# One core of Trainium2, graph attention layer: the last six supersteps of the second edge loop in another order

## The chip, the cores and the metric

The kernel runs on one core of one Trainium2 chip. The time is that of one execution on the device, in microseconds (us). Three executions of the kernel before took 5511.41 us in the median (5510.93 to 5514.28). All times inside the program are counted from the first instruction of one profiled execution.

## What is computed

Two graph layers over 12500 nodes with 64 features and 200000 edges, sorted by destination. The change lies in the second, an attention layer with eight relations:

```python
Z = jnp.einsum('ni,rio->nro', h, fc_weight)
z_s = Z[src, etype]
z_d = Z[dst, etype]
aw = attn_weight[etype, :, 0]
z2 = jnp.concatenate([z_s, z_d], axis=1)
e = jax.nn.relu(jnp.sum(z2 * aw, axis=1))
m = jax.ops.segment_max(e, dst, num_segments=N)
ex = jnp.exp(e - m[dst])
denom = jax.ops.segment_sum(ex, dst, num_segments=N)
alpha = ex / denom[dst]
h_out = jax.ops.segment_sum(alpha[:, None] * z_s, dst, num_segments=N)
```

The first layer is a message layer with `segment_sum` over the same edges. Each layer is followed by an addition of its input and a normalisation.

## The kernel before

The 200000 edges make 1563 tiles of 128. Nodes lie in 98 blocks of 128. Since the edges are sorted, a tile meets one block or a few, and the work is a row of (tile, block) slots, eight to a **superstep**: 208 supersteps (`SO`), 196 groups of eight tiles. Everything is unrolled.

**Gathers.** In each of the two layers GpSimd (POOL) fetches the source rows of each tile by one indirect DMA (`gathers`, L466) into a ring of 184 tiles. It reports each landed group in the semaphore `landed`, and may run on only when the compute side has freed old ring places (`used`, `summed`).

**The second loop** (`phase_layer1`). For the data of superstep s each engine does, in its own fixed program order:

- `onehots(s)` on VectorE (DVE): one-hot matrices of the slots' destinations (L1399, L1401, L1404).
- `scores(s)` on TensorE (PE): sixteen small matmuls (L1340, L1345) into the bank `p_e`; the first L1345 waits for `landed` against a register loaded from the table `xrow`. Then `scores(s)` on DVE (L1410, L1414) makes the logits `ev`.
- `scored(s)` on ScalarE (ACT): one-hot times logit, `ohe` (eight, L1315). `turned(s)` on PE transposes them (eight, L1351) into `p_x`.
- `maxima(s)` on DVE: a reduction (L1424) and a running maximum, split in three bf16 parts `m` (L1427 to L1441). `spread(s)` on PE brings the maxima back to the edges (eight small matmuls, L1357). They land in the last 24 columns of the bank `p_s` of the odd half (`pB`).
- `shifted(s)` on DVE: logit minus maximum, `ed` (L1460, L1462). `weights(s)` on ACT: exponentials and eight weighted one-hots `ohx` (L1305, L1306, L1309).
- `summed(s, h)` on PE: two halves of four f32 matmuls each against the ring (L1366), into `p_s`; `sums(s)` on DVE: eight additions into the accumulator XA (L1454), each waiting for the one ahead of it.

I call a pass of an engine's loop a **turn**. In turn s PE does turned(s-1), scores(s+1), summed(s-3, 0), spread(s-1), summed(s-3, 1). DVE does scores(s), onehots(s+2), then maxima(s-1) and sums(s-4) woven instruction by instruction, then shifted(s-2). ACT does scored(s), weights(s-2). So the data of the last superstep, 207, are added in turn 211.

```python
for s in range(SO + 4):
    if s < SO:
        scores(s)
    if s + 2 < SO:
        onehots(s + 2)
    weave(*([maxima(s - 1)] if 1 <= s <= SO else []), *([sums(s - 4)] if s >= 4 else []))
    if 2 <= s < SO + 2:
        shifted(s - 2)
```

After this loop all engines meet at a barrier, and `phase_out` scales, normalises and stores the result; its first DVE instruction is L1513. The first layer's loop (`phase_layer0`) has the same gathers; there DVE waits for `landed` ahead of L875, against a register of the four that it loads at L899.

Of the kernel before, what the change touches and what calls it, by code (L numbers as in the profile page):

```python
# [17 lines left out]
R = 8  # L18
# [465 lines left out]
def phase_layer0(nc, A):  # L484
# [4 lines left out]
    with ExitStack() as ctx:  # L489
# [268 lines left out]
        def _(e):  # L758
            breg = [e.alloc_register(f"l0vb{j}") for j in range(O)]
            treg = [e.alloc_register(f"l0vt{j}") for j in range(O)]  # L760
            xreg = [e.alloc_register(f"l0vx{j}") for j in range(WX)]
            done = Chain(e, T["dve"])
# [107 lines left out]
            def filled(s):  # L870
                e.wait_ge(S["landed"], e.snap(xreg[0], min_val=1, max_val=TO))
                if s:
                    e.wait_ge(S["pre"], s)
                of, to = e.snap(xreg[1], min_val=0, max_val=RING - O), e.snap(xreg[2], min_val=0, max_val=O)
                e.tensor_tensor(out=full[:, bass.ds(to, O), :], in0=owns, in1=ring[:, bass.ds(of, O), :], op=ALU.add).then_inc(S["full"], 1)  # L875
# [11 lines left out]
            for s in range(SO + 2):  # L887
                if s + 1 < SO:
                    onehots(s + 1)
                if s < SO:  # L890
                    if s:
                        e.wait_ge(S["msg"], s)
                    for h in range(2):
                        e.wait_ge(S[f"m{h}"], s + 1)
                        e.tensor_reduce(out=pT[:, h * H:(h + 1) * H, :], in_=half(h), axis=AXX, op=ALU.add).then_inc(T["dve"], 1)  # L895
                if s >= 2:
                    e.reg_load(breg, A.brow[0:1, (s - 2) * O:(s - 1) * O])
                if s < SO:
                    e.reg_load(xreg, xrow[0:1, s, :])  # L899
                    e.reg_load(treg, wrow[0:1, s, :])  # L900
                    filled(s)
                    take(e, T["dve"], 2)
                for j in range(O):
                    if s >= 2:
                        summed(s - 2, j)
                    if s < SO:
                        added(s, j)
# [341 lines left out]
def phase_layer1(nc, A):  # L1249

    QO, QT, QV = 7, 5, 4
    with ExitStack() as ctx:
# [26 lines left out]
        pE = pb("p1_e", [P, O, 3 * R])  # L1279
# [3 lines left out]
        pB = [pair[1][:, 512 - 3 * O:512].rearrange("p (j c) -> p j c", c=3) for pair in p_s]  # L1283
        names = "oht e ev ohe x m3 b ed ohx s0 s acc dve ex ty landed".split()
# [16 lines left out]
        def _(e):  # L1301
# [16 lines left out]
            for s in range(SO + 2):  # L1318
                if s < SO:
                    scored(s)  # L1320
                if s >= 2:
                    weights(s - 2)

        @block.tensor
        def _(e):
# [3 lines left out]
            xreg = e.alloc_register("l1px")  # L1329

            def scores(s):
                e.reg_load(breg, A.brow[0:1, s * O:(s + 1) * O])
                e.reg_load(treg, trow[0:1, s, :])
                e.reg_load(xreg, xrow[0:1, s, 0:1])
                e.wait_ge(S["oht"], s + 1)
                if s:
                    e.wait_ge(S["ev"], s)
                for j in range(O):
                    b = e.snap(breg[j], min_val=0, max_val=NB)
                    e.matmul(pE[:, j, :], OHT[:, s % QT, j, :], A.S23[:, bass.ds(b, 1), :], start=True, stop=False)  # L1340
                    if j == 0:
                        e.wait_ge(S["landed"], e.snap(xreg, min_val=1, max_val=TO))
# [11 lines left out]
            def spread(s):  # L1354
                e.wait_ge(S["m3"], s + 1)
                for j in range(O):
                    last = e.matmul(pB[s % 2][:, j, :], OHT[:, s % QT, j, :], m3[:, s % 2, j, :], start=True, stop=True)  # L1357
# [12 lines left out]
            for s in range(SO + 3):  # L1370
                if 1 <= s <= SO:
# [3 lines left out]
                if s >= 3:  # L1375
                    summed(s - 3, 0)
                if 1 <= s <= SO:
                    spread(s - 1)
                if s >= 3:
                    summed(s - 3, 1)  # L1380

        @block.vector
        def _(e):
# [74 lines left out]
            def shifted(s):  # L1458
                e.wait_ge(S["b"], s + 1)
                step(e.tensor_reduce(out=md[:, :], in_=pB[s % 2], axis=AXX, op=ALU.add))  # L1460
# [7 lines left out]
            for s in range(SO + 4):  # L1468
# [4 lines left out]
                weave(*([maxima(s - 1)] if 1 <= s <= SO else []), *([sums(s - 4)] if s >= 4 else []))  # L1473
                if 2 <= s < SO + 2:
                    shifted(s - 2)
# [248 lines left out]
```

## Time and profile before

| what | value |
|---|---|
| median of three executions | 5511.41 us |
| span of the profiled execution, first to last instruction | 4190.6 us |
| own time of the profiled execution | not recorded; the median is 1320.8 us more than the span |
| first loop's gathers | 30.7 to 1993.3 us |
| second loop's gathers | 2151.0 to 4106.1 us |
| last addition of the second loop ends | 4153.2 us |
| output phase | 4153.5 to 4190.6 us |
| busy over the span: PE / PE weight loads / DVE / ACT / POOL | 77 / 68 / 71 / 30 / 72 % |
| mean granted TensorE clock | 0.52 of full |

Busy shares are averages over stages with different limits. What counts for a stage is which wait ends last in it. The profile infers who released a wait from semaphore events, and matmul ends are modelled.

### The profile page before, as it was taken

To read this page: it belongs to the slowest core of one execution; us is meant where nothing else is said; L and a number is where in the kernel's file an instruction comes from. 1 tells how busy PE (TensorE), PEld (TensorE's weight loads), DVE (VectorE), ACT (ScalarE), POOL (GpSimd) and SP (SyncE) were. 2 spreads that over 40 slices of the span, in tenths; PEclk is the share of its full clock that TensorE was granted. 3 is DMA by queue.
4 is the path that set the end of the run, shared out by engine and by line. 5 is a ranking of instruction groups with operands and counts; after the bars stand their busy time and mean duration, and the time that the engine had idled before them with its cause. 6 is when DMAs were issued, how large, how long until landed. Compare 5 with 4: busy or idle time off the path is not lost. (4 is left out here: it accounts for less than half of the span.)

```text
span 4190.6 us, 74370 instructions
## 1 busy us (share of the span) xinstructions
PE 3206.3 (77%) x17849; PEld 2851.7 (68%) x17849; DVE 2985.6 (71%) x9486; ACT 1278.0 (30%) x4181; POOL 3029.9 (72%) x3265
## 2 busy tenths in 40 slices
PE   6877677777677777777857877787878888888885
PEld 6766666667666766666626767676777777777774
DVE  6876676677677777777656666676767777777777
ACT  3000000000000000000334544555555555555555
POOL 5777777777777777777257777777777777777773
PEclk6555555555555555555775555555555555555555
DMA  5322222222222222222452222222222222222221
GB/s 187 104 71 71 60 71 71 69 63 72 70 71 72 65 69 71 72 71 62 151 209 59 49 59 49 59 59 59 49 59 59 59 59 49 59 59 59 59 49 37
DMA packets 172566, 300.35 MB, mean 72 GB/s; under 512 B 71720, under 2 KB 78236, under 8 KB 158845
## 3 DMA queue, kind: packets, MB, share of 16 engines
q0 software_dynamic: 100032, 105.03, 12.7%
q1 hardware_dynamic: 43526, 104.29, 6.9%
q10 hardware_dynamic: 28598, 86.26, 6.0%
q8 instruction: 173, 2.83, 0.3%
q14 instruction: 237, 1.93, 0.2%
HBM read 260.36 MB, written 34.99 MB: 70 GB/s over the span
## 5 line engine op out<-in xcount | busy, mean ns | idle before, releaser
L466 POOL DMA_INDIRECT ring<-Btab,idx x1563 | 1485.5, 950 | 504.6 <-issue 338.9
L466 POOL DMA_INDIRECT ring<-Ztab,idx x1563 | 1478.9, 946 | 485.6 <-issue 352.8
L1366 PE MATMUL p_s<-ring,ohx 128*128 x3328 | 806.3, 421 | 160.5 <-issue 157.0
L1366 PEld LDWEIGHTS p_s<-ring,ohx 128*128 128x128 f32 x3328 | 734.7, 325 | 180.8 <-issue 180.8
L754 PEld LDWEIGHTS p_s<-msg,oh 128*128 128x128 f32 x3328 | 726.2, 331 | 99.8 <-issue 99.7
L754 PE MATMUL p_s<-msg,oh 128*128 128x64 f32 x3328 | 756.9, 422 | 48.4 <-ACT msg L648 45.8
L741 PE MATMUL p_m<-A,oht 128*128 x1664 | 436.1, 364 | 411.0 <-DVE full L875 401.7
L648 ACT ACTIVATE msg<-p_t 128x512 f32<-128x512 f32 x208 | 124.2, 597 | 1803.8 <-DVE p_t L881 1790.9
L746 PE MATMUL p_m<-W1c,eaT 65*128 65x128 f32 x1664 | 573.9, 449 | 24.4 <-DMA eaT<-in_eaT_in 24.4
L741 PEld LDWEIGHTS p_m<-A,oht 128*128 128x128 bf16 x1664 | 233.4, 141 | 490.4 <-issue 444.4
L1454 DVE SCALAR_TENSOR_TENSOR XA<-XA,ff,p_s 128x65 f32 x1664 | 468.4, 281 | 129.9 <-DVE XA L1454 73.1
L1424 DVE TENSOR_REDUCE mslot<-p_x 128x8 f32<-128x1024 f32 x208 | 254.7, 1224 | 429.1 <-PE p_x L1351 427.7
L1315 ACT ACTIVATE ohe<-oh,ev 128x128 f32<-128x128 bf16 x1664 | 505.3, 386 | 44.6 <-DVE ev L1414 44.6
L1309 ACT ACTIVATE ohx<-oh,ex 128x128 f32<-128x128 bf16 x1664 | 508.7, 388 | 0.0
L1345 PE MATMUL p_e<-ring,ident_h 128*128 x1664 | 303.4, 196 | 234.2 <-POOLq L453 226.5
L746 PEld LDWEIGHTS p_m<-W1c,eaT 65*128 65x128 f32 x1664 | 455.9, 334 | 33.4 <-DMA eaT<-in_eaT_in 27.7
L875 DVE TENSOR_TENSOR full<-p_m,ring 128x512 f32 x208 | 143.6, 690 | 448.9 <-POOLq L453 430.3
L1351 PE MATMUL p_x<-ident,ohe 128*128 128x128 f32 x1664 | 397.6, 418 | 0.0
L1345 PEld LDWEIGHTS p_e<-ring,ident_h 128*128 128x128 bf16 x1664 | 166.6, 105 | 336.4 <-issue 274.0
L881 DVE TENSOR_TENSOR p_t<-p_t,full 128x64 f32<-128x64 f32 x1664 | 386.2, 233 | 11.7 <-issue 6.3
L868 DVE TENSOR_TENSOR XA<-XA,p_s 128x64 f32 x1664 | 366.9, 221 | 36.2 <-issue 8.5
L895 DVE TENSOR_REDUCE p_t<-p_m 128x256 f32<-128x768 f32 x416 | 379.5, 956 | 13.9 <-PE p_m L746 13.1
(212 smaller groups left out, 3084.4 us busy)
## 6 DMA issues: line engine op xcount, KB each, us to landing
drow<-drow_d SPq DMA_DIRECT2D x53, 1024.0 KB, 5.4
drow<-drow_d ACTq DMA_DIRECT2D x51, 1024.0 KB, 5.2
eaT<-in_eaT_in ACTq DMA_DIRECT2D x208, 128.0 KB
Ztab<-Z_stage SPq DMA_DIRECT2D x49, 536.0 KB, 5.5
ring<-Btab,idx POOLq DMA_INDIRECT x1563
ring<-Ztab,idx POOLq DMA_INDIRECT x1563
xTB<-in_xTB_in SPq DMA_DIRECT2D x7, 448.0 KB, 7.7
Btab<-B_stage SPq DMA_DIRECT2D x7, 448.0 KB, 5.1
```

What stands on the lines that cost most here:

```text
L466: e.indirect_dma_start(out=ring[:, place(t), :], out_offset=None, in_=table[:, :], in_offset=bass.IndirectOffsetOnAxis(ap=idx[:, t:t + 1], ...
L741: e.matmul(parts(j), OHT[:, s % 2, j, :], A.A3[:, bass.ds(b, 1), :].rearrange("p a c -> p (a c)"), start=True, stop=True)
L746: last = e.matmul(own(j // 2), eaT[:, s % QE, j // 2, :], A.W1c2[:, :], start=True, stop=True)
L754: last = e.matmul(pS[r % 2][:, j, :], OH[:, r % QO, j, :], msg[:, r % 2, j, :], start=True, stop=True)
L881: ins = e.tensor_tensor(out=pT[:, j:j + 1, :], in0=pT[:, j:j + 1, :], in1=full[:, bass.ds(t, 1), :], op=ALU.add)
L895: e.tensor_reduce(out=pT[:, h * H:(h + 1) * H, :], in_=half(h), axis=AXX, op=ALU.add).then_inc(T["dve"], 1)
L1309: ins = e.activation(OHx[:, o, j, :], OH[:, s % QO, j, :], ACT.Copy, scale=ex[:, o, j:j + 1])
L1315: ins = e.activation(OHe[:, s % 2, j, :], OH[:, s % QO, j, :], ACT.Relu, scale=ev[:, s % QV, j:j + 1])
L1345: last = e.matmul(pE[:, j, :], A.ident_h[:, :], part.unsqueeze(2).to_broadcast([P, 3, R]), start=False, stop=True)
L1351: last = e.transpose(pX[:, j, :], OHe[:, s % 2, j, :], A.ident[:, :])
L1366: last = e.matmul(pS[s % 2][h][:, j % 4, :], OHx[:, s % 2, j, :], ring[:, bass.ds(t, 1), 0:D + 1], start=True, stop=True)
L1454: e.scalar_tensor_tensor(out=acc, in0=acc, scalar=ff[:, s % QV, j:j + 1], in1=pS[s % 2][j // 4][:, j % 4:j % 4 + 1, :], op0=ALU.mult, op1= ...
```

## The change

**Order.** `END = SO - 6` = 202. Up to turn 201 nothing moves. From turn 202 on, sums, their matmuls and their weights run one superstep closer behind the scores:

- DVE: in turn 202 sums(198) alone first. In each turn then shifted(s-2), scores(s), onehots(s+2), and maxima(s-1) woven with sums(s-3). The last turn is 210.
- ACT: weights(s-2) ahead of scored(s), where it stood behind it.
- PE: turn 202 has summed(199) and summed(200), from there summed(s-2). In turns 208 and 209 both halves of summed(s-2) stand together, in turn 208 behind spread(207).
- From data 201 on, spread writes to free columns of the bank of `p_e`, and shifted reads them there.

**Registers.** In both loops the count that `landed` is compared with is first copied to a register of its own (REGISTER_ALU): on DVE in the first loop, on PE in the second, once a superstep, 208 each.

```diff
@@ phase_layer0, DVE
+            landed = e.alloc_register("l0vn")
...
-                e.wait_ge(S["landed"], e.snap(xreg[0], min_val=1, max_val=TO))
+                e.wait_ge(S["landed"], e.snap(landed, min_val=1, max_val=TO))
...
                     e.reg_load(xreg, xrow[0:1, s, :])
+                    e.reg_alu(landed, xreg[0], 0, ALU.max)
                     e.reg_load(treg, wrow[0:1, s, :])
@@ phase_layer1
+    END = SO - 6
-        pE = pb("p1_e", [P, O, 3 * R])
+        p_e = ctx.enter_context(nc.psum_tensor("p1_e", [P, 512], F32))
+        pE = p_e[:, 0:O * 3 * R].rearrange("p (a b) -> p a b", b=3 * R)
+        pBE = p_e[:, O * 3 * R:O * 3 * R + 3 * O].rearrange("p (j c) -> p j c", c=3)
+        spreads = lambda s: pB[s % 2] if s < END - 1 else pBE
@@ ACT
             for s in range(SO + 2):
+                if s >= END:
+                    weights(s - 2)
                 if s < SO:
                     scored(s)
-                if s >= 2:
+                if 2 <= s < END:
                     weights(s - 2)
@@ PE
                 e.reg_load(xreg, xrow[0:1, s, 0:1])
+                e.reg_alu(landed, xreg, 0, ALU.max)
...
+            for s in range(END, SO + 2):
+                if s <= SO:
                     turned(s - 1)
                 if s + 1 < SO:
                     scores(s + 1)
-                if s >= 3:
-                    summed(s - 3, 0)
-                if 1 <= s <= SO:
+                if s == END:
+                    for h in range(2):
+                        summed(s - 3, h)
+                if s < SO:
+                    summed(s - 2, 0)
+                if s <= SO:
                     spread(s - 1)
-                if s >= 3:
-                    summed(s - 3, 1)
+                if s >= SO:
+                    summed(s - 2, 0)
+                summed(s - 2, 1)
@@ DVE
+            for s in range(END, SO + 3):
+                if s == END:
+                    for _ in sums(s - 4):
+                        pass
+                if s < SO + 2:
+                    shifted(s - 2)
                 if s < SO:
                     scores(s)
                 if s + 2 < SO:
                     onehots(s + 2)
-                weave(*([maxima(s - 1)] if 1 <= s <= SO else []), *([sums(s - 4)] if s >= 4 else []))
-                if 2 <= s < SO + 2:
-                    shifted(s - 2)
+                weave(*([maxima(s - 1)] if s <= SO else []), sums(s - 3))
```

**DVE at the end of the loop, before.** In the rows below L1460 and L1462 are shifted, each L1444 opens a group of eight additions (a load of eight registers, then pairs of L1452 and L1454, of which the first is shown).

```order
L1460 TENSOR_REDUCE md<-p_s 128x8 [waits l1_b]
L1462 SCALAR_TENSOR_TENSOR ed<-ev,md 128x8 [waits l1_ty]
L1444 TENSOR_LOAD tabs
L1452 ISA [waits l1_acc,l1_s0]
...
L1460 TENSOR_REDUCE md<-p_s 128x8 [waits l1_b]
L1462 SCALAR_TENSOR_TENSOR ed<-ev,md 128x8 [waits l1_ty]
L1444 TENSOR_LOAD tabs
L1452 ISA [waits l1_acc,l1_s0]
...
L1444 TENSOR_LOAD tabs
L1452 ISA [waits l1_acc,l1_s0]
...
L1252 UNCONDITIONAL_BRANCH
```

Here sums(205) stands between shifted(206) and shifted(207), and sums(206) and sums(207) follow. The same place in the changed program:

```order
L1484 TENSOR_REDUCE md<-p_e 128x8 [waits l1_b]
L1486 SCALAR_TENSOR_TENSOR ed<-ev,md 128x8 [waits l1_ty]
L1468 TENSOR_LOAD tabs
L1476 ISA [waits l1_acc,l1_s0]
...
L1468 TENSOR_LOAD tabs
L1476 ISA [waits l1_acc,l1_s0]
...
L1255 UNCONDITIONAL_BRANCH
```

The shift shown is shifted(207): only two groups of additions are left behind it, sums(206) and sums(207). shifted(206) has moved ahead of maxima(207).

**PE at the same place, changed.** L1361 is turned(207), L1367 spread(207), L1376 summed.

```order
L1361 MATMUL p_x<-ident,ohe 128x128 [waits l1_ohe]
L1361 MATMUL p_x<-ident,ohe 128x128 x7
L1367 MATMUL p_e<-m,oht 128x3 [waits l1_m3]
L1367 MATMUL p_e<-m,oht 128x3 x7
L1372 TENSOR_LOAD tabs
L1375 ISA [waits l1_ohx]
L1376 MATMUL p_s<-ring,ohx 128x65
```

Before, the first half of summed(205) stood between turned(207) and spread(207), its second half behind, and summed(206) and summed(207) followed; now only summed(206) and summed(207) follow.

**DVE at the seam, turn 202, changed.** The last of eight additions of sums(198), then shifted(200), scores(202) and the one-hots.

```order
L1476 ISA [waits l1_acc]
...
L1484 TENSOR_REDUCE md<-p_s 128x8 [waits l1_b]
L1486 SCALAR_TENSOR_TENSOR ed<-ev,md 128x8 [waits l1_ty]
L1434 TENSOR_TENSOR prod<-p_e,ty 128x192 [waits l1_oht,l1_e]
L1438 TENSOR_REDUCE ev<-prod 128x8 [waits l1_ty]
L1423 TENSOR_TENSOR oh<-p_iota,dstl 128x1024
```

Before, the scores (L1410, L1414) opened the turn, and sums(198) was woven with maxima(201).

## Rows read from the trace of the kernel before

**Rows 1.** Windows: busy us (instructions) of PE, PEld, DVE, ACT, POOL; granted clock; DMA.
```profile
2151.00:4106.00 1955.00, 1548.15 (x9767) 1381.52 (x9767) 1366.27 (x4724) 1023.34 (x3661) 1478.74 (x1563) 0.51 0.23 57
4106.00:4153.50 47.50, 36.84 (x218) 34.18 (x218) 28.91 (x115) 23.13 (x84) 0.12 (x1) 0.50 0.01 2
4153.50:4190.60 37.10, 0.00 (x0) 0.00 (x0) 31.82 (x46) 20.10 (x57) 23.98 (x12) 0.50 0.38 86
```
**Rows 2.** POOL, gathers: count, min/median/max ns, first to last start; then the last.
```profile
L466 POOL DMA_INDIRECT ring<-Ztab,idx x1556: 940/944/1205, 2159.8 to 4105.2; - x195
...
L466 POOL DMA_INDIRECT ring<-Ztab,idx x23: 940/944/947, 4077.7 to 4105.2; - x23
...
4105.18 0.94 POOL L466 DMA_INDIRECT ring<-Ztab,idx  x1 [0.30 <-DVE XA L1454]
```
**Rows 3.** Waits over the second loop, then one over the first: us, times, longest.
```profile
PE p_e L1345 <- POOLq L453: 226.5, 129, 5.8
...
POOL ring L466 <- DVE XA L1454: 73.1, 240, 0.3
...
DVE full L875 <- POOLq L453: 430.3, 156, 4.3
```
**Rows 4.** Timeline of PE in the last turns: start, us, instruction, idle before it.
```profile
4080.82 1.91 PE L1351 MATMUL p_x<-ident,ohe 128*128 128x128 f32 x8
...
4094.09 0.20 PE L1345 MATMUL p_e<-ring,ident_h 128*128 x1 [1.37 <-POOLq L453]
...
4100.79 1.91 PE L1351 MATMUL p_x<-ident,ohe 128*128 128x128 f32 x8
...
4104.02 0.20 PE L1345 MATMUL p_e<-ring,ident_h 128*128 x1 [1.30 <-POOLq L453]
...
4110.79 1.91 PE L1351 MATMUL p_x<-ident,ohe 128*128 128x128 f32 x8
...
4112.49 0.23 PE L1340 MATMUL p_e<-S,oht 128*128 x1
...
4114.28 1.96 PE L1366 MATMUL p_s<-ring,ohx 128*128 x8 [0.79 <-issue]
...
4118.13 1.91 PE L1351 MATMUL p_x<-ident,ohe 128*128 128x128 f32 x8
...
4133.33 1.91 PE L1351 MATMUL p_x<-ident,ohe 128*128 128x128 f32 x8
...
4138.68 0.37 PE L1357 MATMUL p_s<-m,oht 128*128 128x3 bf16 x8 [1.02 <-DVE m L1441]
...
4143.13 3.67 PE L1366 MATMUL p_s<-ring,ohx 128*128 x16 [2.26 <-ACT ohx L1309]
...
4147.58 3.67 PE L1366 MATMUL p_s<-ring,ohx 128*128 x16 [0.78 <-ACT ohx L1309]
```
**Rows 5.** Timeline of DVE in the same stretch.
```profile
4102.74 1.23 DVE L1424 TENSOR_REDUCE mslot<-p_x 128x8 f32<-128x1024 f32 x1 [2.60 <-PE p_x L1351]
...
4135.28 1.22 DVE L1424 TENSOR_REDUCE mslot<-p_x 128x8 f32<-128x1024 f32 x1 [2.44 <-PE p_x L1351]
...
4140.09 0.17 DVE L1462 SCALAR_TENSOR_TENSOR ed<-ev,md 128x8 f32<-128x8 f32 x1
...
4140.95 0.28 DVE L1454 SCALAR_TENSOR_TENSOR XA<-XA,ff,p_s 128x65 f32 x1 [0.69 <-issue]
...
4144.55 0.17 DVE L1462 SCALAR_TENSOR_TENSOR ed<-ev,md 128x8 f32<-128x8 f32 x1
...
4149.71 0.28 DVE L1454 SCALAR_TENSOR_TENSOR XA<-XA,ff,p_s 128x65 f32 x1 [0.83 <-PE p_s L1366]
...
4152.90 0.28 DVE L1454 SCALAR_TENSOR_TENSOR XA<-XA,ff,p_s 128x65 f32 x1 [0.16 <-DVE XA L1454]
```
**Rows 6.** Timeline of ACT: the last weighting.
```profile
4144.99 2.44 ACT L1309 ACTIVATE ohx<-oh,ex 128x128 f32<-128x128 bf16 x8
```
**Rows 7.** Timeline of DVE: the last superstep of the first loop.
```profile
2005.39 0.69 DVE L875 TENSOR_TENSOR full<-p_m,ring 128x512 f32 x1 [0.66 <-issue]
```

More of the change, by code:

```diff
@@ L1329, in _ @@
             xreg = e.alloc_register("l1px")
+            landed = e.alloc_register("l1pn")
             def scores(s):
@@ L1341, in scores @@
                     if j == 0:
-                        e.wait_ge(S["landed"], e.snap(xreg, min_val=1, max_val=TO))
+                        e.wait_ge(S["landed"], e.snap(landed, min_val=1, max_val=TO))
                     t = e.snap(treg[j], min_val=0, max_val=RING - 1)
@@ L1356, in spread @@
                 for j in range(O):
-                    last = e.matmul(pB[s % 2][:, j, :], OHT[:, s % QT, j, :], m3[:, s % 2, j, :], start=True, stop=True)
+                    last = e.matmul(spreads(s)[:, j, :], OHT[:, s % QT, j, :], m3[:, s % 2, j, :], start=True, stop=True)
                 last.then_inc(S["b"], 1)
@@ L1369, in _ @@
             scores(0)
-            for s in range(SO + 3):
-                if 1 <= s <= SO:
+            for s in range(END):
+                if s:
+                    turned(s - 1)
+                scores(s + 1)
+                if s >= 3:
+                    summed(s - 3, 0)
+                if s:
+                    spread(s - 1)
+                if s >= 3:
+                    summed(s - 3, 1)
+            for s in range(END, SO + 2):
+                if s <= SO:
                     turned(s - 1)
@@ L1374, in _ @@
                     scores(s + 1)
-                if s >= 3:
-                    summed(s - 3, 0)
-                if 1 <= s <= SO:
+                if s == END:
[4 more added lines that the diff above has]
+                if s <= SO:
                     spread(s - 1)
-                if s >= 3:
-                    summed(s - 3, 1)
+                if s >= SO:
+                    summed(s - 2, 0)
+                summed(s - 2, 1)
         @block.vector
@@ L1459, in shifted @@
                 e.wait_ge(S["b"], s + 1)
-                step(e.tensor_reduce(out=md[:, :], in_=pB[s % 2], axis=AXX, op=ALU.add))
+                step(e.tensor_reduce(out=md[:, :], in_=spreads(s), axis=AXX, op=ALU.add))
                 stepped()
@@ L1467, in _ @@
             onehots(1)
-            for s in range(SO + 4):
+            for s in range(END):
+                scores(s)
+                onehots(s + 2)
+                weave(*([maxima(s - 1)] if s else []), *([sums(s - 4)] if s >= 4 else []))
+                if s >= 2:
+                    shifted(s - 2)
[4 more added lines that the diff above has]
+                if s < SO + 2:
+                    shifted(s - 2)
                 if s < SO:
```

## Prediction

> **What bounds the kernel now.** I read the windows by stage first, then the gathers, the waits, and last the timelines of the final turns, engine by engine. The windows give three stretches that matter: 1955 us in which the second loop's gathers run, 47.5 us of the loop behind the last gather, and 37.1 us of output [rows 1]. In the first, POOL is the bound: 1563 gathers in 1955 us are 1.251 us each, 0.944 us of work and some 0.30 us of issue, so eight take 10.0 us [rows 1, 2]. POOL waits for the additions 240 times, and never for more than those 0.3 us [rows 3]; nothing the compute side does sets its pace. PE, in turn, waits 226.5 us in this loop for landed groups, and DVE 430.3 us in the first loop [rows 3]. The timeline of PE shows the same at the end: transposes start 10.0 us apart (4100.79, 4110.79; two turns earlier 4080.82), with 1.30 to 1.37 us of waiting for a landed group in a turn, the last one at 4104.02 [rows 4]. From there the pace is that of the compute engines: the next transposes are 7.34 us apart (4110.79, 4118.13) [rows 4]. So a paced turn has 10.0 - 7.34 = 2.66 us to spare on PE. DVE has as much: it sits idle 2.60 us ahead of the maxima [rows 5].
>
> The last maxima start at 4135.28 [rows 5]. Behind them come only leftovers of the pipeline: two shifts, and sums(205), (206) and (207), one after the other on DVE, until 4152.90 + 0.28 = 4153.18 [rows 5]. Only the stretch behind the last landed group can give the change anything.
>
> **Term 1, the end of the loop: a gain of 4.3 us.** The last chain before is: shift(207) at 4144.55, ScalarE's one-hots from 4144.99 (2.44 us), summed(207) on PE from 4147.58, first addition at 4149.71, last end 4153.18 [rows 4 to 6]. Shift(207) stood behind sums(205) because that group lay between the two shifts. The group with its load of registers and the shift costs 4144.55 - 4140.09 = 4.46 us [rows 5]. In the new order sums(205) is woven with maxima(207), in the place where sums(204) was, and shift(206) stands ahead of maxima(207), where DVE was idle for 2.44 us [rows 5] and the shift of some 0.4 us fits. So shift(207) lands at about 4140.09, where shift(206) was, and the whole chain moves up 4.46 us, if PE is free for it. PE is nearly the limit: spread(207) starts at 4138.68 as before and takes some 0.25 us until the next may start; then come a load of registers, which stands in the open for about 0.79 us [rows 4], and both halves of a superstep's sums, 3.67 us to the last end and some 3.5 until the next may start [rows 4]. That is 4138.68 + 0.25 + 0.79 + 3.5 = 4143.2 for the end of summed(206). The weights of 207 are there at 4144.99 + 2.44 - 4.46 = 4143.0 [rows 6]. PE then starts summed(207) at 4143.2 to 4143.3 if the second load of registers hides behind the matmuls; from there to the first addition it takes 4149.71 - 4147.58 = 2.13 us, and eight additions 4153.18 - 4149.71 = 3.47 us [rows 4, 5]: end at 4148.9. The gain is 4.3 us; 3.5 if the second load stands in the open as well. I take 4.3, since behind eight f32 transposes PE's next matmul starts at 4112.49 without a gap, loads and all [rows 4].
>
> **Term 2, the seam: a loss of 0.1 us.** Turn 202 gets work twice. On PE an extra summed: 3.5 us and a load of 0.79 make 4.3. On DVE the additions of sums(198), 3.47 us, stand alone ahead of the shift and the scores; of a shift there is no more than before in any turn. PE has 2.66 us to spare in each of the turns 203 and 204, 5.3 us together, before the last group for which it waits has landed at 4104.02, and 4.3 is less. DVE has its 2.60 us of idle time in the same two turns, 5.2 us against 3.47 [rows 5]. So turned(204) should start at 4110.79 again and maxima(203) a little later than 4102.74. Since each of the two waits for the other while both are late, a rest may stay. I count 0.1. Bounds: nothing, or the whole extra 4.3 if none of it is caught up.
>
> **Term 3, the tail's five turns: nothing.** The pace of 7.34 us is PE's own: the same matmuls in the same order, with another superstep's number on the sums. The new order asks ScalarE for weights(s-2) ahead of scored(s): twice eight activations of 2.44 us together [rows 6] and two small ones, some 5.2 us a turn, under 7.34. From the end of the maxima over spread (0.25), shift (0.4), weights (2.7) and half a sum (1.75) to the next spread is 5.1 us of work, under 7.34 too. The waits that stay are for the maxima.
>
> **Term 4, the register copies: a loss of 0.2 us.** 208 on DVE in the first loop and 208 on PE in the second. No row shows a copy. From below: it gains nothing, as nothing is taken away. From above: a load of eight registers in the open, which costs 0.66 us on DVE and 0.79 on PE [rows 4, 7]; a copy that has to wait for its load can make at most such a gap. In the paced turns any of these lies in PE's 1.3 us and DVE's wait for a landed group [rows 3, 4]. Not covered are the last two supersteps of each loop, four copies: 0 to 3.0 us. A single register operation is nearer to the small steps between matmuls than to a load, so I take 0.05 each.
>
> **Sum.** -4.3 + 0.1 + 0 + 0.2 = -4.0 us. The barrier and the output phase behind it move up unchanged, since DVE's last addition is what the barrier waits for. The sum is made against the one profiled span: 4190.6 becomes 4186.6. That execution's own time isn't recorded; the 1320.8 us between the span and the median of 5511.41 lie outside the program's instructions and I leave them as they are. Forecast: 5507.4 us. A measurement of this kernel can tell 0.2%, or 11 us, from no change; this gain is 0.07%.
>
> **Rivals.** (a) **The seam isn't caught up**, because DVE's burst also holds up the gathers. Against it: the 23 gathers from 4077.7 to 4105.2 took 940 to 947 ns each with additions, reductions and one-hots running beside them, and the longest in the loop was 1205 ns [rows 2]. The group landed at 4104.02 would come later by what the eight moved additions cost, at most 8 x 0.28 = 2.2 us; with the seam's own delay the gain falls to between 0 and 3 us: 5508.5 to 5511.5. The Trainium skill's page "SBUF — State Buffer" ("SBUF: two separate sides") has a rule for this: VectorE and GpSimd share a port pair under an exclusive lock, and GpSimd can't write descriptors of its DMAs while VectorE holds it. By that rule POOL would be held up; the 940 to 947 ns in this trace show no such hold.
>
> (b) **The register copy makes PE wait for its loads in every superstep**, the one that ends slower. PE's scores of each superstep would then sit out a fixed c, ahead of the landed wait. PE's cover is 226.5 us over some 201 supersteps, 1.13 us each [rows 3]. Below that nothing happens but in the tail; above it PE takes over from POOL as the bound of the loop, at (c - 1.13) x 201. At c = 1.3 that is +34 us, less 4: 5541. It decides at c = 1.15, where the loss is as large as the gain. Against it: the load of eight registers shows 0.79 us [rows 4], and PE waits for its first block register at that place today already. The Trainium skill's page "Runtime: NRT & Kernel Launch" ("Instruction fetch mechanics") puts a register load at about 200 ns a register: 17 registers would be 3.4 us, and by it the kernel would be far slower. The 0.79 us for eight in this trace, with the issue in it, is under 0.1 each.
>
> (c) **Nothing changes**, since another chain sets the end. The barrier waits for all engines, but PE's last sixteen matmuls are through at 4147.58 + 3.67 = 4151.25, ahead of DVE's last addition, and POOL has been idle since 4106 [rows 2, 4, 5]. Then 5511.4.
>
> (d) **The tail gets faster by a turn**: one turn less at 7.34 us would be 5504. Against it: the turns up to the last maxima are as many as before; only leftovers go.
>
> **Chances.** Forecast, 3 to 4.5 us gained: 0.70. (a): 0.14. (b), with over 11 us lost: 0.03. (c): 0.06. (d): 0.04. Others, such as code that lies elsewhere after 416 more instructions: 0.03. Range: the forecast's bounds reach from 5507.0 to 5508, rivals (a) and (c) to 5511.5, (d) to 5504; the three executions before lie between 0.5 us under and 2.9 us over their median. That makes 5503.5 to 5512.5. Faster by over 0.2% would need 11 us, more than all the tail's leftovers of one superstep: 0.02. Slower by over 0.2% is (b) and a bit: 0.04. Same: 0.94.
>
> **What the new profile would show.** The last gather starts at 4105.2 again, within 1 us; else (a). The last group that PE waits for is released at about 4104, and the last maxima start at 4135.3, within 0.5 us: seam caught up. In turn 202 eight additions stand alone ahead of a shift, at 4079 to 4083. Behind the last maxima: one shift at 4140.1, then two groups of additions, the last beginning at about 4145.4 and ending at 4148.9; summed(206) and summed(207) almost without a gap on PE. PE's waits for landed groups in the second loop stay near 226 us, or fall by under 10; if they fall by half or more, the copies cost. I am wrong if the last maxima come later than 4137, or if the wait for landed groups is gone.

## The result, and the profile after

The changed kernel took **5535.18 us** (median of 4 executions, 5529.65 to 5541.09), the kernel before, run beside it, 5511.17 us. The ratio is **1.0046**, 95% interval 1.0035 to 1.0058: 24 us slower, by more than 0.2% and outside my range. The profiled execution took 5529.65 us itself and its span is 5527.9 us. So 1.75 us lie around the program, not the 1320.8 us that I had left outside it. Beside [rows 1], its windows (us; then busy us and instructions of PE, PEld, DVE, ACT, POOL; granted clock; DMA): the second loop's start, POOL's pause behind it, the rest of the gathers, and the loop behind the last gather.

```profile
2938.00:3166.00 228.00, 20.28 (x128) 15.69 (x128) 21.64 (x46) 13.75 (x43) 172.33 (x182) 0.50 0.19 37
3166.00:3230.00 64.00, 35.39 (x249) 33.20 (x249) 34.73 (x122) 25.22 (x90) 0.00 (x0) 0.50 0.05 18
3230.00:5330.00 2100.00, 1283.43 (x8701) 1167.83 (x8700) 1198.54 (x4216) 909.92 (x3263) 1305.31 (x1379) 0.51 0.20 47
5330.00:5490.00 160.00, 133.90 (x911) 124.10 (x909) 125.28 (x453) 97.56 (x351) 0.00 (x0) 0.53 0.04 15
```

The gathers of both loops, beside [rows 2]: count, min/median/max ns, first to last start.

```profile
L466 POOL DMA_INDIRECT ring<-Btab,idx x1563: 942/947/2037, 30.7 to 2638.7; - x196
L466 POOL DMA_INDIRECT ring<-Ztab,idx x1563: 942/947/1210, 2935.0 to 5326.8; - x196
```

One gather is as long as before (947 ns), the granted clock the same (0.51). Yet the first loop's gathers last 2608 us instead of 1963, the second's 2392 instead of 1955, and 160 us of the loop lie behind the last gather, not 47.5. By e1 and e3 below, this is not the effect of the change: the profile that I was shown came from a chip on which the same program is faster. Its waits (us, times, longest), beside [rows 3]:

```profile
POOL ring L466 <- issue: 773.9, 2526, 1.2
POOL ring L466 <- remote: 359.9, 172, 2.3
POOL ring L466 <- DVE XA L869: 345.9, 87, 5.3
POOL ring L466 <- SPq L443: 290.8, 158, 3.2
```
```profile
DVE oh L853 <- remote: 940.1, 88, 12.4
DVE mslot L1448 <- remote: 875.5, 174, 42.4
DVE full L876 <- POOLq L453: 2.0, 1, 2.0
```
```profile
PE p_e L1355 <- POOLq L453: 2.3, 1, 2.3
```

POOL now really waits for the compute side. The waits for landed groups in which I had hidden the copies, 226.5 us on PE and 430.3 on DVE [rows 3], are gone: 2.3 and 2.0 us. "remote" here is a wait that ended with a semaphore event, but so long behind every instruction that could have caused it that the view names none. The timeline at the second loop's start shows it: PE, then DVE.

```profile
2981.15 0.20 PE L1355 MATMUL p_e<-ring,ident_h 128*128 x1
3002.87 0.37 PE L1367 MATMUL p_s<-m,oht 128*128 128x3 bf16 x8 [21.51 <-issue]
3003.10 1.95 PE L1361 MATMUL p_x<-ident,ohe 128*128 128x128 f32 x8
3045.43 0.20 PE L1350 MATMUL p_e<-S,oht 128*128 x1 [40.39 <-issue]
```
```profile
3044.43 0.36 DVE L1434 TENSOR_TENSOR prod<-p_e,ty 128x192 f32<-128x192 f32 x1 [41.62 <-remote]
...
3089.24 1.22 DVE L1448 TENSOR_REDUCE mslot<-p_x 128x8 f32<-128x1024 f32 x1 [42.40 <-remote]
```

The transposes of 3003.10 end at 3005.05, and the event that DVE waits for is recorded at 3089.21. DVE, idle for 41.6 us, takes up the scores 63 us after PE's last score matmul (2981.35 to 3044.43), and, idle for another 42.4, the maxima 84 us after the transposes (3005.05 to 3089.24), while POOL issues gather after gather. Later, in the steady part, POOL and DVE:

```profile
4010.36 0.94 POOL L466 DMA_INDIRECT ring<-Ztab,idx  x1 [0.30 <-issue]
4013.41 0.95 POOL L466 DMA_INDIRECT ring<-Ztab,idx  x1 [2.10 <-remote]
```
```profile
4013.26 1.22 DVE L1448 TENSOR_REDUCE mslot<-p_x 128x8 f32<-128x1024 f32 x1 [4.59 <-remote]
```

PE's transposes for those maxima had ended at 4008.76 by the same trace, but DVE starts within 0.15 us of POOL's restart, behind 2.1 us without a gather. Eight gathers of 1.25 us and one such pause make the turn of some 12 us (11.6 to 12.0 from 3900 to 4019 us). In the unpaced turns behind the last gather it is 7.3 to 7.9 us.

### The profile page after: what moved, and what is told of

Read it like the earlier page. It is cut to its first block and busy times, and to the rows that moved or that the text cites. A ratio compares the mean times of both kernels' runs of the same rounds, so it can differ in the third digit from the quotient of the medians.

```text
span 5527.9 us, 74786 instructions
## 1 busy us (share of the span) xinstructions
PE 3115.1 (56%) x17849; PEld 2801.3 (51%) x17849; DVE 2984.1 (54%) x9486; ACT 1278.0 (23%) x4181; POOL 3032.0 (55%) x3265
## 5 line engine op out<-in xcount | busy, mean ns | idle before, releaser
L754 PE MATMUL p_s<-msg,oh 128*128 128x64 f32 x3328 | 785.0, 409 | 755.7 <-issue 719.4
L754 PEld LDWEIGHTS p_s<-msg,oh 128*128 128x128 f32 x3328 | 752.7, 325 | 806.4 <-issue 805.4
L1376 PE MATMUL p_s<-ring,ohx 128*128 x3328 | 811.1, 421 | 184.1 <-issue 184.1
L1376 PEld LDWEIGHTS p_s<-ring,ohx 128*128 128x128 f32 x3328 | 740.4, 326 | 208.0 <-issue 207.5
L853 DVE TENSOR_TENSOR oh<-p_i,dstl 128x1024 f32<-128x1024 f32 x208 | 253.6, 1219 | 948.3 <-remote 940.1
L1350 PE MATMUL p_e<-S,oht 128*128 x1664 | 216.1, 191 | 391.3 <-issue 348.3
L1361 PE MATMUL p_x<-ident,ohe 128*128 128x128 f32 x1664 | 397.8, 418 | 0.8 <-issue 0.8
L1355 PE MATMUL p_e<-ring,ident_h 128*128 x1664 | 220.9, 186 | 286.0 <-issue 282.8
```

Source lines behind the costliest of these rows:

```text
L754: last = e.matmul(pS[r % 2][:, j, :], OH[:, r % QO, j, :], msg[:, r % 2, j, :], start=True, stop=True)
L1361: last = e.transpose(pX[:, j, :], OHe[:, s % 2, j, :], A.ident[:, :])
L1376: last = e.matmul(pS[s % 2][h][:, j % 4, :], OHx[:, s % 2, j, :], ring[:, bass.ds(t, 1), 0:D + 1], start=True, stop=True)
```

## Experiments

The cores came from several chips, each with the kernel before run beside: its median was 4192 us on one of them, 5512, 5513 and 5513 on three, 5575 and 5601 on two. I call these levels. Each ratio is against the kernel before on the same chip.

**Copies alone, and the changed kernel, at the 4192 level.** `e1_copies_only` has the old order and the copies of the diff in both loops; `e2_copies_three` has each of them three times in its source, both engines (VectorE's shown); `e3_changed_again` is the changed kernel.

```diff
@@ e2, against e1
                     e.reg_alu(landed, xreg[0], 0, ALU.max)
+                    e.reg_alu(landed, xreg[0], 0, ALU.max)
+                    e.reg_alu(landed, xreg[0], 0, ALU.max)
```

> The kernel before with only the 416 register copies; the order of the last six supersteps is the old one. Theory A (the copies cost the 24 us, some 0.06 us each, since the compute engines and not the gathers set the pace in the timed executions): 5530 to 5537 us, ratio 1.004 to 1.005. Theory B (the new order costs it, at the seam or in the tail): 5509 to 5514, ratio 1.000. The profile should also tell whether a kernel in the old order spans 4191 us, as the profile of before did, or some 5510 us with stretches in which PE sits idle on nothing that the profile shows, as in the changed kernel's.

> As the first, with each copy made three times (1248 in all instead of 416). Theory A: the cost grows with the number, to three times that of the first, about +70 us over the kernel before. Theory B: within 3 us of the first.

> The changed kernel unchanged, on the same chip. Both theories: ratio 1.0046 again, 5530 to 5540 us. Against the first run it gives the cost or gain of the order alone: theory A says equal to it or up to 4 us less; theory B says 20 to 26 us more.

Measured: 4192.53, 4192.62 and 4187.64 us against 4191.86; ratios 1.0000 and 1.0000 (each 0.9991 to 1.0009), and 0.9989 (0.9980 to 0.9998). So at this level the copies cost nothing that can be told, and the change gains 4.2 us (0.8 to 8). Of three copies e2 says nothing: its trace holds 74786 instructions, exactly as e1's does, 416 more than the kernel before (74370). Two of three equal copies, each of which only writes the same value again, aren't in the compiled program. The same holds for e10 and e17 below. The changed kernel's timeline there, PE and DVE, answers [rows 4, 5]:

```profile
4080.21 1.91 PE L1361 MATMUL p_x<-ident,ohe 128*128 128x128 f32 x8
4087.02 5.38 PE L1376 MATMUL p_s<-ring,ohx 128*128 x24 [0.76 <-issue]
...
4094.19 1.91 PE L1361 MATMUL p_x<-ident,ohe 128*128 128x128 f32 x8
...
4101.56 1.91 PE L1361 MATMUL p_x<-ident,ohe 128*128 128x128 f32 x8
...
4138.59 7.25 PE L1376 MATMUL p_s<-ring,ohx 128*128 x32 [0.41 <-issue]
```
```profile
4134.40 1.23 DVE L1448 TENSOR_REDUCE mslot<-p_x 128x8 f32<-128x1024 f32 x1 [2.44 <-PE p_x L1361]
...
4139.14 0.17 DVE L1486 SCALAR_TENSOR_TENSOR ed<-ev,md 128x8 f32<-128x8 f32 x1
...
4148.04 0.28 DVE L1478 SCALAR_TENSOR_TENSOR XA<-XA,ff,p_s 128x65 f32 x1 [0.16 <-DVE XA L1478]
```

Turn 202 is 14.0 us long (4080.21 to 4094.19), and the last maxima still come 29.8 us behind the last gather's start (4104.6), before 30.1: the seam is caught up. The last addition ends 13.9 us behind the start of the last maxima (4148.32 - 4134.40), before 17.9 [rows 5].

**The order at the 5601 level.** `e4_old_order` is the kernel of e1; `e5_end3` and `e6_end14` are the changed kernel with a shorter and a longer new stretch (`SO - 3` and `SO - 14`).

```diff
-    END = SO - 6
+    END = SO - 3
```

> The old order with the copies again. Its time against the kernel before tells which of the two levels this chip shows. If 4190 us: ratio 1.000, as the first run. If 5510 us: by theory C (at that level the copies cost nothing either, the 24 us are the seam and the tail, where the compute engines run behind the gathers and have no slack to catch up in) 5509 to 5514; by theory A (copies) 5530 to 5537; and its profile shows PE stopping in every superstep while gathers run.

> The changed kernel with the switch three supersteps before the end instead of six (turn 205), behind the last group that PE waits for. My working: the extra sums of the turn of the switch, 4.3 us on PE, then find no slack; from the trace's steps I get a loss of 2 us against the old order, where the switch in turn 202 gains 4. At the 4190 level: 4193 to 4195 us, ratio 1.0005. If the seam were free, 4187.6 as with the changed kernel. At the 5510 level theory C expects the same as, or a little more than, the changed kernel.

> The switch fourteen supersteps before the end (turn 194), in the midst of the gathers. At the 4190 level the seam lies further inside the slack: 4187 to 4188 us, as the changed kernel or up to 1 us better. At the 5510 level, theory C: no better than the changed kernel, since there the compute engines run behind throughout and a seam costs the same wherever it stands.

Measured against 5601.43: 5610.38 (1.0016, 1.0005 to 1.0028), 5615.47 (1.0023, 1.0014 to 1.0033) and 5619.05 us (1.0036, 1.0024 to 1.0048). In the traces the seam's turn is 14.7 us in e5 and 15.3 in e6, where its neighbours are 7.3 to 8.0, and from the start of the last transposes to the end of the last addition it is 15.9 and 16.0 us instead of 19.8 in e4. At this level some 18 turns are left when the last gather has been issued, so that the seam lies in unpaced turns in e5 and e6 alike: it costs 7 to 8 us, and the end gives back 4. But the old order with copies is 9 us above the kernel before as well (3 to 16), so the order isn't all of it.

**Old order, changed kernel, a gentler seam, and sixteen copies on PE in the source, at the 5513 level.** `e7_old_order` and `e8_changed` are the two kernels again. In `e9_gentle_seam` VectorE does the scores ahead of the lone additions in turn 202, and ScalarE moves its weights one turn later; `e10_pe16` has the old order with PE's copy sixteen times in its source.

```diff
@@ e9, DVE
                 if s == END:
+                    scores(s)
                     for _ in sums(s - 4):
                         pass
@@ e10, PE
-                e.reg_alu(landed, xreg, 0, ALU.max)
+                for _ in range(16):
+                    e.reg_alu(landed, xreg, 0, ALU.max)
```

> The anchor of this comparison: the old order with the copies. On a chip of the 4190 level 1.000 of the kernel before. On one of the 5500 to 5600 level 1.000 to 1.003, as in the fourth run; what the next runs differ from it by is the order's part alone.

> The changed kernel. Level 4190: 4 us less than the old order. Level 5500: theory C (PE has no slack there, the turn of the switch costs 8 us and the end gives back 4) says 3 to 5 us more than the old order with the copies; theory A (all is in the copies) says 0 to 4 us less.

> The changed kernel with another turn 202: DVE does scores(202) ahead of the lone sums(198), and ACT scored(202) ahead of weights(200), so that PE's next scores need not wait 3.3 us for the logits. Level 4190: as the changed kernel, within 1 us. Level 5500: 2 to 3 us less than the changed kernel, so about the old order's time, since the pace there is PE's own.

> The old order, but PE's copy of each superstep in the second loop made sixteen times (3120 instructions more on PE's queue alone). Level 4190: PE has 1.1 us of slack a superstep; at a few hundredths of a us each fifteen copies fit in it, ratio 1.000 (theory E: a copy costs up to 0.1 us, then 0.4 us a superstep over the slack, +80 us). Level 5500, where PE's semaphore updates reach DVE only once the gathers pause: if each PE instruction adds to what has to be worked off in that pause (theory D), +30 to +140 us; if only the pause's length counts, under 15 us.

Measured against 5513.0: 5532.72 (1.0035, 1.0021 to 1.0048), 5531.35 (1.0036, 1.0022 to 1.0050), 5532.22 (1.0038, 1.0025 to 1.0052) and 5538.26 us (1.0051, 1.0035 to 1.0066). Two things follow. The copies in the old order already cost 20 us, about the whole loss of the change. The order adds nothing that can be told: from the last gather's start to the end of the span it is 201.4 us in e8 and 198.2 in e7, 3 us more, which drowns in the few us between executions. The gentler seam makes turn 202 11.6 us long, not 15.7, and that stretch 198.1 us; the time is the same. What a copy costs when there are more of them e10 can't tell, since its program has 74786 instructions, as e7's has. PE's copy in e7, and then all that is left in e10 of the sixteen (count; min/median/max ns):

```profile
L1338 PEldq ALU_OP  x208: 32/33/47, 2947.5 to 5465.5; - x104
```
```profile
L1339 PEldq ALU_OP  x208: 32/33/47, 2942.7 to 5459.8; - x104
```

So e10 is a repetition of e7, and the second loop's gathers take as long in both (2392.2 and 2393.1 us).

**Which copy.** `e11_old_order_2` is the anchor (old order, both copies). `e12_const_first` has a constant as the count in the first loop, so only PE's copy; `e13_const_second` the other way round. The constant is never under what the register holds, and binds nowhere here, since the gathers are far ahead of the compute side (the wait for landed groups is 2 us in the whole loop). `e14_late_copy` puts VectorE's copy behind the load of the slot registers. The compiled programs differ by more than the copies: with the constant, VectorE's move of the count (one MOVE a superstep) is gone too in e12, and in e13 PE's move and its load of the count, which nothing uses any more. In e14 the copy and the move have become one instruction.

```diff
@@ e12, DVE, first loop (e13: PE, second loop)
-                e.wait_ge(S["landed"], e.snap(landed, min_val=1, max_val=TO))
+                e.wait_ge(S["landed"], min(s + 1, TO))
...
-                    e.reg_alu(landed, xreg[0], 0, ALU.max)
@@ e14
                     e.reg_load(xreg, xrow[0:1, s, :])
-                    e.reg_alu(landed, xreg[0], 0, ALU.max)
                     e.reg_load(treg, wrow[0:1, s, :])
+                    e.reg_alu(landed, xreg[0], 0, ALU.max)
```

> The old order with the register copies in both loops, as anchor for the three beside it. Where the kernel before takes about 5510 us: 1.0035 of it (19 us more), as in the earlier run of this kernel; where it takes about 4190: 1.0000.

> Old order; in the first loop VectorE waits for the constant min(s + 1, 196) in place of a register, without a copy; in the second PE has its copy. At the 5510 level: theory 'VectorE's copy costs': 1.000, within 0.001, of the kernel before; theory 'PE's copy costs': 1.0035. At the 4190 level the constant makes the last dozen supersteps of the first loop wait for the last group: up to 50 us more, of no meaning for the copies.

> Old order; in the second loop PE waits for the constant, without a copy; in the first VectorE has its copy. At the 5510 level: theory 'VectorE's copy costs': 1.0035; theory 'PE's copy costs': 1.000. If both this and the one with the constant in the first loop come out near 1.0035, neither copy is the cause, but something that all of them share against the kernel before, such as where code and tables lie. At the 4190 level up to 50 us more, as above.

> Old order with both copies, but VectorE's copy in the first loop stands behind the load of the eight slot registers instead of ahead of it, so that the two loads go out together. If VectorE's copy costs because it holds back the second load, the ratio at the 5510 level falls from 1.0035 to 1.001 or less; if the copy's place is indifferent, 1.0035. At the 4190 level 1.000 either way.

Measured against 5512.84: e11 5533.83 (1.0036, 1.0022 to 1.0050); e12 5511.81 (0.9997, 0.9988 to 1.0006); e13 5524.01 (1.0023, 1.0013 to 1.0032); e14 5518.71 us (1.0010, 1.0001 to 1.0019). Without VectorE's copy and move 22 us go, without PE's copy, move and load 10 (the intervals of e11 and e13 overlap), with VectorE's copy late and merged into the move 15; each difference is good to some 8 us. More code as such is not what costs: the program of e13 has 208 instructions fewer than the kernel before (74162 against 74370) and is 11 us slower. The waits of VectorE and of POOL in the first loop, e11:

```profile
DVE p_t L882 <- issue: 74.3, 96, 1.2
DVE XA L869 <- issue: 52.9, 124, 1.1
DVE full L876 <- issue: 35.5, 49, 1.6
...
POOL ring L466 <- DVE XA L869: 349.4, 87, 5.7
```

The same of e12:

```profile
DVE p_t L881 <- issue: 26.5, 62, 1.0
DVE XA L868 <- issue: 21.1, 51, 1.2
DVE full L875 <- issue: 18.5, 28, 1.4
...
POOL ring L466 <- DVE XA L868: 326.2, 87, 5.6
```

VectorE stands in the open, waiting for nothing but its own instruction stream, for 162.7 us in e11, 66.1 in e12 and 92.1 in e14. These gaps lie ahead of the additions that free ring places, and there POOL waits 87 times. But the sum of the gaps is no measure of the copy's price: it is 206.7 us in e13, whose first loop is e11's, 388 to 415 at the 5601 level (e4 to e6), and 183.2 in e18 below, which has no copy at all and is the fastest. The length of the gathers repeats better: the first loop's take 2612.3 us in e11, 2612.1 in e13, 2583.4 in e12 and 2603.9 in e14. (The profiled execution of e12 was 10.6 us under its median, so that 28.9 us between e11 and e12 is too much.) One stall in e11, VectorE then POOL (e12's gap ahead of `full` at the same place is nothing):

```profile
2111.68 1.22 DVE L853 TENSOR_TENSOR oh<-p_i,dstl 128x1024 f32<-128x1024 f32 x1 [11.01 <-remote]
...
2115.44 0.69 DVE L876 TENSOR_TENSOR full<-p_m,ring 128x512 f32 x1 [0.40 <-issue]
```
```profile
2111.85 0.95 POOL L466 DMA_INDIRECT ring<-Btab,idx  x1 [2.98 <-SPq L443]
2116.95 0.95 POOL L466 DMA_INDIRECT ring<-Btab,idx  x1 [4.15 <-DVE XA L869]
```

VectorE's queue shows what a copy does there, in e11 and then, merged with the move, in e14:

```profile
L901 DVEq ALU_OP  x208: 45/45/58, 180.0 to 2793.7; - x104
```
```profile
L902 DVEq FUSED_REGOPS  x208: 94/94/94, 181.9 to 2784.9; - x104
```

The loads run one after the other in every run: with nothing between them the load of the slot registers starts 0.03 us behind the end of the load of `xreg`, with the copy between them 0.11 us (medians of 208 supersteps, e14 and e11). From the end of the load of `xreg` to the addition into `full` the median is 1.35 us in e11, 1.33 in e14 and 1.27 in e12. So VectorE's copy between the loads holds the next load back by 0.08 us a superstep, an estimate of 17 us over 208 if nothing hides it. The late copy shortens the way to `full` by 0.03 us only, an estimate of 5 us. The 15 us that were measured for e14 are more than that, and their error of some 8 us just doesn't reach it.

e13 takes 6.3 us from the second loop's gathers (2386.1 us against 2392.4) and 5.7 from what lies behind them. How the 21 us of e11 divide between the two copies is not shown, as the constants took more than the copies away.

**Loads and copy at the head of the superstep; sixteen copies on VectorE in the source.** `e15_early_old` and `e16_early_new` move the three loads and the copy ahead of the one-hots, in the old and the new order. `e17_dve16` has the old order and VectorE's copy sixteen times in its source.

```diff
@@ e15, e16
             for s in range(SO + 2):
+                if s >= 2:
+                    e.reg_load(breg, A.brow[0:1, (s - 2) * O:(s - 1) * O])
+                if s < SO:
+                    e.reg_load(xreg, xrow[0:1, s, :])
+                    e.reg_alu(landed, xreg[0], 0, ALU.max)
+                    e.reg_load(treg, wrow[0:1, s, :])
                 if s + 1 < SO:
                     onehots(s + 1)
@@ e17
-                    e.reg_alu(landed, xreg[0], 0, ALU.max)
+                    for _ in range(16):
+                        e.reg_alu(landed, xreg[0], 0, ALU.max)
```

> Old order, both copies; in the first loop VectorE's three register loads and its copy stand at the head of the superstep, ahead of the one-hots, where they can run while VectorE waits. The copy's own time between the reduction and the addition into 'full' is gone: at the 5510 level ratio 0.996 to 1.000 (the loads' remaining gaps of some 0.1 us each leave the stretch that POOL waits for, too); the rival, that the copy costs wherever it stands, says 1.0035. At the 4190 level 1.000.

> The same in the changed order (END = SO - 6). At the 5510 level 1 to 2 us off the run beside it, which can't be told apart; at the 4190 level 0.999, 4 us less than the kernel before. If this is faster than both kernels at the 5510 level, it is the version to keep.

> Old order, VectorE's copy in the first loop sixteen times in its old place. If each copy costs its own time on the path (20 us over 104 pairs of supersteps for one), sixteen cost far more than one: over 1.01 at the 5510 level. If only the first copy costs, because it waits for its load, near 1.004 as with one, as on PE. At the 4190 level: 1.000 unless fifteen more copies exceed VectorE's wait for landed groups, some 2 us a superstep.

Measured against 5511.92: 5553.61 (1.0073, 1.0060 to 1.0086), 5551.76 (1.0068, 1.0055 to 1.0081) and 5533.86 us (1.0032, 1.0021 to 1.0043). The sixteen copies of e17 are one again in its trace:

```profile
L902 DVEq ALU_OP  x208: 45/45/58, 180.4 to 2792.8; - x104
```

So e17, like e10, is the old order with one copy a superstep. Together e7, e10, e11 and e17 are four runs of it on three chips of this level: 20, 25, 21 and 22 us above the kernel before. Both of my expectations for e15 failed. Its first loop's gathers do get shorter (2601.4 us), but from there to the second loop's first gather it takes 332.1 us instead of 299.5. VectorE behind the last gather, e15 and then e11:

```profile
2663.34 1.23 DVE L853 TENSOR_TENSOR oh<-p_i,dstl 128x1024 f32<-128x1024 f32 x1 [1.96 <-issue]
...
2672.29 1.23 DVE L853 TENSOR_TENSOR oh<-p_i,dstl 128x1024 f32<-128x1024 f32 x1 [1.96 <-issue]
```
```profile
2666.79 1.22 DVE L853 TENSOR_TENSOR oh<-p_i,dstl 128x1024 f32<-128x1024 f32 x1
...
2673.76 1.21 DVE L853 TENSOR_TENSOR oh<-p_i,dstl 128x1024 f32<-128x1024 f32 x1
```

Three loads and a copy with nothing beside them stand in the open for 1.96 us, and the superstep shown grows from 6.97 to 8.95 us. Twenty supersteps start behind the last gather in both runs; their mean is 7.3 us in e11 and 9.0 in e15, which makes the 32.6 us. In their old place the loads run while the reductions do. The two runs are 1.9 us apart, as said for the order.

**Neither copy, new order.** `e18_constants` is the changed kernel with the constant in both loops, and without the load for the count in the second. Its trace has 73746 instructions, 624 fewer than the kernel before: two moves and a load in each of 208 supersteps.

```diff
@@ DVE, first loop, and PE, second loop
-                e.wait_ge(S["landed"], e.snap(landed, min_val=1, max_val=TO))
+                e.wait_ge(S["landed"], min(s + 1, TO))
@@ PE
-                e.reg_load(xreg, xrow[0:1, s, 0:1])
-                e.reg_alu(landed, xreg, 0, ALU.max)
```

> The changed order, with the constant min(s + 1, 196) as the count in both loops: no copies, and in the second loop no load for the count. At the 5510 level the differences measured so far add up to 5533.8 - 22.0 (first loop) - 9.8 (second loop) - 1.4 (order) = 5500.6 us, ratio 0.998: faster than both kernels. If the two differences overlap, 5511, ratio 1.000. At the 4190 level the last dozen supersteps of each loop wait for the last group: 1.01 or more, slower than both.

Measured: 5554.67 us against 5575.39 on the same chip, ratio 0.9965 (0.9952 to 0.9978). It is 21 us (12 to 27) faster than the kernel before at this level. The changed kernel wasn't timed beside it; near 5510 it lost 0.36 to 0.46% to the kernel before. My sum was made at the 5513 level; its 0.998 lies at the edge of the interval. It wasn't run at the 4192 level, where I expect it to be slower.

## Why the prediction was wrong

**The step that failed** is the sentence on the difference between median and span: "the 1320.8 us between the span and the median of 5511.41 lie outside the program's instructions and I leave them as they are". They lie inside. The profile was of the 4192 level (span 4190.6 us), the times of the 5510 level, and every row that I argued from, with its covers, held for the former alone. A quarter of the time unexplained by the span should have made the profile suspect.

**Term 4, the register copies (+0.2, at most 3.0).** This is the term of the sum that failed with it. It was right at the 4192 level: ratio 1.0000 in e1. At the level of the times it was 20 to 25 us (e7, e10, e11, e17). I had covered the copies by the waits for landed groups; there those waits are 2 us long, and the cover is gone. The size of one wasn't wrong: 20 us over 416 copies are 0.05 us each, the figure that I took. What was too low was the number of uncovered copies, four.

**Term 1, the end of the loop (-4.3).** Nearly right at both levels. At the 4192 level the span from the last maxima to the last addition fell by 4.0 us; shift(207) starts at 4139.14 and summed(206) and (207) run as one group of 32 matmuls. In the profile after, the same: the last additions, DVE.

```profile
5481.24 0.17 DVE L1486 SCALAR_TENSOR_TENSOR ed<-ev,md 128x8 f32<-128x8 f32 x1
5482.82 0.28 DVE L1478 SCALAR_TENSOR_TENSOR XA<-XA,ff,p_s 128x65 f32 x1 [1.42 <-PE p_s L1376]
...
5490.15 0.28 DVE L1478 SCALAR_TENSOR_TENSOR XA<-XA,ff,p_s 128x65 f32 x1 [0.16 <-DVE XA L1478]
```

**Term 2, the seam (+0.1).** Right at the 4192 level, for the reason given: paced turns followed it in which it was made up (14.0, 7.4 and 8.8 us, together as long as three turns of 10). In the profile after it lies twelve unpaced turns behind the last gather, and nothing catches it up:

```profile
5421.25 1.91 PE L1361 MATMUL p_x<-ident,ohe 128*128 128x128 f32 x8
5429.79 5.38 PE L1376 MATMUL p_s<-ring,ohx 128*128 x24 [0.76 <-issue]
...
5436.97 1.91 PE L1361 MATMUL p_x<-ident,ohe 128*128 128x128 f32 x8
```

15.7 us where 7.3 to 7.9 is the rule: 8 us, above the 4.3 that I had as the upper bound. In e9, where VectorE's scores no longer wait for the lone additions, the turn is 11.6 us, 4 too many, which is PE's extra sums alone: the bound held for one engine, and in the changed order the two extras come one after the other.

**Term 3, the tail's turns (nothing).** Right: 7.3 to 7.9 us behind the seam, old order and new.

**The rivals.** (b) came nearest, but not as I had it. The slowdown comes with the register copies on engines that another waits for, yet on VectorE in the first loop at least as much as on PE in the second, and without the threshold of 1.13 us. (a) failed at the 4192 level, where the gathers lasted 1954.4 us with the seam; the seam that isn't caught up did happen at the other level, without holding up a gather, since none was left. (c) and (d) have nothing for them: the chain moved as Term 1 said, no turn was saved. The upper end of my range doesn't follow from its terms either: 5511.5 and 2.9 make 5514.4, not 5512.5. The measured 5535.18 lies beyond both. The two rules of the Trainium skill that I weighed are answered as well. In e15 the 20 registers of three loads and a copy take 1.96 us in the open, about 0.1 us a register. By the Trainium skill's page "Runtime: NRT & Kernel Launch" ("Instruction fetch mechanics"), 200 ns a register, an estimate is 4.0 us, so the measurement decides against it here. The gathers took 944 to 947 ns in the median at both levels, and POOL's longer waits end with an addition or an update, not in a longer gather. The Trainium skill's page "SBUF — State Buffer" ("SBUF: two separate sides") ties the lock to VectorE's operations in a mode with two ports or with two inputs in SBUF; the hold isn't seen in these gathers, and no run tells in which mode VectorE's operations ran.

The marks for a new profile held in e3, counted from the last gather's start: the last maxima come 29.8 us behind it, where I had 30.1, and PE's wait for landed groups is 228.6 us. (By the clock all of it is 0.6 to 0.9 us early, since the second loop's gathers start at 2150.2 and not at 2151.0.) In the profile after, that wait was gone, as I had named for being wrong.

## What to carry to other kernels

Set the span of a profiled execution against the measured median before reading anything else: if they don't agree within a few us, the covers read from its waits are not those of the timed executions, and each cost that was set to nothing for their sake needs a price without them. Where an engine has no wait to hide in, even an instruction of 45 ns in every superstep shows: 416 of them cost 20 us here. Keep register loads in a place where a long instruction runs beside them (1.96 us a superstep in the open otherwise), and compare with a constant where one does (e18). When an experiment repeats an instruction to price it, count it in the trace: three runs here had one where the source had three or sixteen. A seam between two orders belongs where the later turns still have slack, and where that is depends on how far the gathers run ahead.

## What the hardware showed that I had not expected

The same changed kernel took 4187.64 us on one chip and 5531.35 on another, at 0.52 of the clock on both and with 944 to 947 ns a gather. What differs is how long it takes until VectorE and POOL go on after PE has finished: 84 us at the second loop's start, while 182 gathers were issued without a pause, and 4.5 us in the steady turn shown (4008.76 to 4013.26), up to the next pause of POOL. At the 4192 level VectorE takes up the scores 0.04 us after PE's last one (2184.18) at the same place, with gathers running:

```profile
2184.22 0.36 DVE L1434 TENSOR_TENSOR prod<-p_e,ty 128x192 f32<-128x192 f32 x1 [5.07 <-PE p_e L1355]
```

Of five other chips none was at the 4192 level. That the gathers hold the updates up is my reading of this timing; no run took the gathers away to show it, and why one chip is free of it stays open.

A register copy takes 33 ns on PE and 45 ns on VectorE, and the move that stands ahead of a wait on a register 36 ns on VectorE; taking the moves out as well, and one load, made e18 faster than the kernel before.

What stays open: how the 21 us divide between the two copies, why e14 saves more than the 0.03 us a superstep that its queue shows, why the copies cost only 9 us (3 to 16) at the 5601 level, what more than one copy would cost, and how much of the gain of e18 is the load that it leaves out.
